# A fused conditional mixing and MXFP4 FFN kernel: 64 x 64 mixing quarters, ScalarE on tile pairs, and a new order on every engine

## The reference

```python
w = weights[conditions]                       # [64, 64, 64]
y = einsum('bct,bcd->bdt', x, w)              # fp32
def quant(x):                                 # blocks of 32 along the last axis
    amax  = max(abs(xb), axis=-1)
    scale = exp2(floor(log2(amax)) - 2)
    q     = clip(xb / scale, -6, 6)
    lsb   = where(|q| < 2, 0.5, where(|q| < 4, 1.0, 2.0))
    return round(q / lsb) * lsb * scale
out = x + einsum('mk,nk->mn', quant(y), quant(W)) + bias    # K = N = 512
```

## Time and profile before

| | us |
|---|---|
| median of three runs | 104.99 |
| the three runs | 103.79, 104.99, 107.01 |
| the profiled execution | 105.2 |
| its span, first to last instruction | 103.7 |
| last residual add starts | 100.39 |
| mean granted TensorE clock | 0.918 of 2.4 GHz |

### The profile page before, as it was taken

How to read it: one execution, slowest core, us unless ns; L and a number is a source line. 1 busy time by engine, 2 the same in 40 slices (tenths; PEclk the granted TensorE clock), 3 DMA queues, 4 the chain that set the end, 5 groups by cost and what they waited for, 6 DMA issues and landing times.

```text
span 103.7 us, 1697 instructions
## 1 busy us (share of the span) xinstructions
PE 82.4 (79%) x434; PEld 40.8 (39%) x440; DVE 91.6 (88%) x149; ACT 79.0 (76%) x113; POOL 28.6 (28%) x50
## 2 busy tenths in 40 slices
PE   5991799904399987996999699699969944899970
PEld 4970334501363435343534534263443413253420
DVE  3579999999996689999999999999999999999660
ACT  3840299869774999999999999999999997903400
POOL 3368999664485203000300300030020003000000
PEclk9999859999556999999999999999999998558999
DMA  2898989999998840967994696689387775949855
GB/s 29 313 340 200 340 229 397 344 275 307 318 230 280 292 149 20 234 179 282 236 190 173 231 190 120 242 239 206 127 299 152 152 270 172 213 102 339 328 209 197
DMA packets 13820, 23.70 MB, mean 229 GB/s; under 512 B 3815, under 2 KB 4339, under 8 KB 13812
## 3 DMA queue, kind: packets, MB, share of 16 engines
q1 hardware_dynamic: 11508, 17.83, 50.7%
q0 software_dynamic: 2016, 5.26, 24.9%
q10 hardware_dynamic: 288, 0.52, 1.9%
HBM read 10.49 MB, written 8.39 MB: 182 GB/s over the span
## 4 chain that ended last, share of the span: by engine, by line
DVE 63%; PE 18%; issue 6%; DMA 5%; ACT 4%; SPq 1%; DVEq 0%; ACTq 0%
DVE n_int L507 14%; DVE a L528 9%; DVE top L519 9%; DVE low L494 7%; PE o_ps L268 5%; DMA w_sb<-in_L_ffn_weight_dram 5%; DVE m L455 4%; PE y_ps L244 4%; DVE inv L499 4%; PE y_ps L268 3%; DVE m L461 3%; PE o_ps L257 2%; DVE amax L472 2%; DVE s L478 2%; DVE s L489 2%
## 5 line engine op out<-in xcount | busy, mean ns | idle before, releaser
L244 PE MATMUL y_ps<-x_sb,mix 128*128 128x512 f32 x64 | 33.5, 658 | 6.2 <-ACT y_sb L357 3.4
L268 PE MATMUL o_ps<-wT,aT 128*128 128x512 bf16 x106 | 26.7, 399 | 0.5 <-issue 0.3
L365 ACT ACTIVATE zone<-inv 128x2048 int16<-128x2048 int16 (+1 forms) x10 | 17.4, 1746 | 5.9 <-DVE inv L499 5.8
L349 ACT ACTIVATE z<-y_ps 128x512 bf16<-128x512 bf16 x32 | 18.7, 625 | 2.7 <-PE y_ps L244 2.2
L244 PEld LDWEIGHTS y_ps<-x_sb,mix 128*128 128x128 f32 x64 | 12.7, 210 | 18.5 <-issue 17.6
L157 POOL DMA_DIRECT2D mix<-in_L_cond_weights_dram x32 | 17.1, 539 | 9.7 <-issue 8.6
L507 DVE TENSOR_TENSOR n_int<-y_sb,inv 128x1024 int16<-128x1024 f32 x16 | 19.0, 1222 | 0.8
L227 POOL DMA_DIRECT2D x_sb<-o_sb x6 | 5.3, 880 | 47.5 <-ACT o_sb L373 47.5
L357 ACT COPY y_sb<-y_ps 128x512 f32<-128x512 f32 x32 | 18.1, 605 | 0.0
L268 PEld LDWEIGHTS o_ps<-wT,aT 128*128 128x128 bf16 x112 | 10.7, 101 | 14.5 <-issue 4.1
L257 PE MATMUL o_ps<-ident,a 128*128 128x128 bf16 x128 | 9.3, 231 | 8.4 <-DVE a L528 8.4
(11 more groups left out here) (39 smaller groups left out, 56.0 us busy)
## 6 DMA issues: line engine op xcount, KB each, us to landing
x_sb<-in_x_dram SPq DMA_DIRECT2D x7, 1024.0 KB, 6.9
x_sb<-o_sb POOLq DMA_DIRECT2D x6, 768.0 KB, 5.7
out_dram<-x_sb SPq DMA_DIRECT2D x6, 768.0 KB, 3.5
out_dram<-x_sb SPq DMA_DIRECT2D x14, 256.0 KB, 2.6
x_sb<-in_x_dram SPq DMA_DIRECT2D x2, 512.0 KB, 6.5
w_sb<-in_L_ffn_weight_dram ACTq DMA_DIRECT2D x2, 256.0 KB, 2.9
w_sb<-in_L_ffn_weight_dram SPq DMA_DIRECT2D x2, 256.0 KB, 4.3
mix<-in_L_cond_weights_dram POOLq DMA_DIRECT2D x32, 16.0 KB, 4.8
```

Source lines behind the costliest of these rows:

```text
L244: nc.tensor.matmul(y_ps[:, t, :], mix[:, (step - 1) * GROUP + t, :], x_tiles(step, t), start=True, stop=True).then_inc(y_ready, 1)
L268: last = nc.tensor.matmul(o_bank(step, t), aT[:, t, c, :], wT[:, c, :], start=False, stop=(c == KC - 1))
L349: nc.scalar.activation(blocked(z[:, step % 2, t, :]), permuted_high(y_ps[:, t, :]), ACT.Abs, scale=ZONE_GAIN).then_inc(z_ready, 1)
L365: nc.scalar.activation(zone[:, t0:t0 + n, :].bitcast(I16), inv[:, t0:t0 + n, :].bitcast(I16), ACT.Copy, bias=float(EXPONENT), scale=-1.0). ...
```

## The change

1. **Mixing.** `mix` holds only the 64 x 64 matrices, without cleared corners. `mix_pair` makes four products of 64 x 64 for each pair of tiles, one on each quarter of the array; results of the off-diagonal quarters land in the other half of the partitions, so within a pair of tiles two samples change places. The transposes of `turn_pair` put them back, by writing their columns in 2 x 64 pieces.
2. **ScalarE** takes z and y in pairs of tiles, 1024 elements. All quantisation tensors are laid out by sub-block first, then tile. In the loop the turned copies come last, and the first copy out comes right behind the zone.
3. **VectorE.** `highest_zone` is gone; its limit comes from `lowest_zone` (the constants move by two binades, and W's scale factor from 0.25 to 4). The tree of step s+1 is interleaved with the rounding of step s, and the add stands behind `lowest_zone`.
4. **FFN.** `ffn_pair` starts as soon as the first two tiles are turned, with two bias matmuls each time. Both mixing pairs follow, before the transposes.
5. **Prologue.** 24 warm-up rounds, the bias loaded as 16 x 32 by GpSimd, its four small VectorE steps set among those of W, twelve one-row transfers instead of four of three rows, and no memsets of `mix`.
6. **Tail.** The residual of step 7 is added on TensorE: `residual_pair` multiplies x by an identity, again in quarters, into the bank of the output. ScalarE copies the result to `x_sb` and the store puts exchanged samples right. Step 8 does not exchange. VectorE adds step 8 alone.

No matmul is put in to keep TensorE busy while it waits.

```diff
-                nc.tensor.matmul(y_ps[:, t, :], mix[:, (step - 1) * GROUP + t, :], x_tiles(step, t),
-                                 start=True, stop=True).then_inc(y_ready, 1)
+        QUARTERS = ((0, 0), (1, 1), (0, 1), (1, 0))
+        HALVES = (slice(0, C), slice(C, P))
...
+                for i, (r, g) in enumerate(QUARTERS):
+                    n = 2 * q + g
+                    mixed = y_ps[HALVES[r], n, :] if step == LAST else y_ps[HALVES[g], 2 * q + r, :]
+                    last = nc.tensor.matmul(mixed, mix[HALVES[r], (step - 1) * GROUP + n, :],
+                                            x_tiles(step, n)[HALVES[r], :], start=True, stop=True)
+            def residual_pair(step, q):
+                for r, g in QUARTERS:
+                    nc.tensor.matmul(o_bank(step, 2 * q + r)[HALVES[g], :], ident_f[HALVES[r], :],
+                                     x_tiles(step, 2 * q + g)[HALVES[r], :], start=True, stop=False)
+            def ffn_pair(step, q):
+                pe.wait_ge(aT_ready, tiles_done(step, 2 * q + 1))
+                if q == 0 and 1 < step < LAST - 1:
+                    pe.wait_ge(added, adds_before(step))
+                for t in (2 * q, 2 * q + 1):
+                    bias_tile(step, t, start=(step != LAST - 1))
+                for t in (2 * q, 2 * q + 1):
+                    ffn_tile(step, t)
...
-                highest_zone(step + 3)
...
+                nc.vector.tensor_tensor(a2[:, t:t + n, :].rearrange("p t (h k) -> p h t k", h=HI),
+                                        columns(n_int, t, n).rearrange("p h (t k) -> p h t k", k=COLS),
+                                        columns(top, t, n).rearrange("p h (t k) -> p h t k", k=COLS), ALU.mult
...
-            nc.gpsimd.memset(mix[C:P, 2 * GROUP:TILES, 0:C], 0.0).then_inc(lower_clear, 1)
-            nc.gpsimd.memset(mix[0:C, 2 * GROUP:TILES, C:P], 0.0).then_inc(upper_clear, 1)
...
+            copy_late(0)
+            copy_turned_last(0)
+            copy_turned_last(1)
+            copy_late(1)
+            copy_turned_last(2)
+            copy_turned_last(3)
```

More of the change, by code:

```diff
@@ L278, in ffn_group, with keep_busy @@
                     ffn_tile(step, t)
+            def keep_busy(times):
+                for i in range(times):
+                    c = i % KC
+                    nc.tensor.matmul(o_ps[:, 2, c * P:(c + 1) * P], idle[:, :], idle[:, :], start=True, stop=True)
             pe.wait_ge(idle_ready, 1)
             with pe.Fori(0, WARMUPS) as _:
[L282 to L285 removed]
@@ L525, in rescale @@
+            def rescale(step, done, rounded, t=0, n=GROUP):
+                if step > 0 and t == 0:
                     dve.wait_ge(t_ready, GROUP * step)
@@ L574, in _ @@
             rescale(0, 1, 2)
-            tree_1(1, 3)
-            tree_2(3)
-            tree_3(3)
+            tree_1(1)
+            tree_2(4)
+            tree_3(4)
             block_max(3)
             lowest_zone(3)
-            highest_zone(3)
-            lift(1, 3)
-            top_zone(2)
+            lift(1, 3).then_inc(z_used, 1)
+            top_zone(3)
             invert(2)
             for step in range(1, LAST):
+                if step > 1:
+                    tree_1(step + 1)
@@ L599, in _ @@
-                lift(step + 1, step + 3)
-                top_zone(step + 2)
-                invert(step + 2)
-            for half in range(2):
-                round_y(LAST, half)
-                limit(LAST, LAST + 1 + half, 2 * half, 2)
-                rescale(LAST, LAST + 1 + half, 2 * LAST + 1 + half, 2 * half, 2)
-            for step in DVE_STEPS:
-                for t in range(GROUP):
-                    add_residual(step, t)
+                if step == 1:
+                    tree_1(step + 1)
+                    limit(step, step + 1)
+                    tree_2(step + 4)
+                    rescale(step, step + 1, 2 * step + 2)
+                    tree_3(step + 4)
+                    block_max(step + 3)
+                    lowest_zone(step + 3)
+                else:
+                    tree_3(step + 4)
+                    limit(step, step + 1)
+                    block_max(step + 3)
+                    rescale(step, step + 1, 2 * step + 2)
+                    lowest_zone(step + 3)
+                    add_residual(step - 1, 0)
@@ L612 @@
+                lift(step + 1, step + 3).then_inc(z_used, 1)
+                top_zone(step + 3)
+                invert(step + 2)
+            for q in range(2):
+                round_y(LAST, q)
+                limit(LAST, LAST + 1 + q, 2 * q, 2)
+                rescale(LAST, LAST + 1 + q, 2 * LAST + 1 + q, 2 * q, 2)
+            for t in range(GROUP):
+                add_residual(LAST, t)
 _INS = ["x", "itok_B_1_198", "L0_cond_weights", "L0_ffn_weight", "L0_ffn_bias"]
```

500 lines of the change are left out of this document (243 added, 257 removed).

## The result

The changed kernel takes **108.63 us** (median of 4 runs, 108.04 to 109.89), the kernel before 104.96 beside it (4 runs, 103.79 to 107.01): a ratio of 1.037, 95% interval 1.022 to 1.052. Forecast was 103.6 us, a little faster than before. It is slower, by 3.7%; the stated range of 99 to 113 holds the time, but the change went the other way. Some executions of every kernel here come out one to four per cent longer at a lower granted clock; the ratios leave them out and the medians do not, so a ratio can differ from the quotient of two medians.

What follows compares the result with a forecast made beforehand. It took VectorE and ScalarE as full before, and a 9.64 us ScalarE-TensorE loop after. 105.2 less 4.0 gave 101.2, 101.0 at the median; plus 2.6 for the clock made 103.6 us, range 99 to 113.

Steps and rivals of the forecast that it cites:

- The loop: Steady step through ScalarE and TensorE, from turned copy through FFN and copies to the next: 9.64 us, 0.35 more than before.
- Quartered mixing: TensorE's mixing in 64 x 64 quarters: between 0.86 us a pair and 3.87 us for two pairs; the lower bound was taken.
- the forecast's case: Quarters run side by side on TensorE, clock lost now and then: 103.6 us, between 101.5 and 106, chance 0.38.
- The second rival: TensorE's quarters go in order, two at a time, so the loop runs through mixing at 11.27 us: 112.8 us, chance 0.22.
- 28.7 + 5 x 9.64: Start of step 6's first turned copy: step 1's at 28.7 us plus five equal loops, 76.9 us against 77.3 before.
- Sum at full clock: 96.4 - 100.39: Shift in the start of the last residual add, -4.0 us, taken off the profiled execution's 105.2 to give 101.2.
- The clock: TensorE's rests of 2.2 us a step lose the clock one and a half times at 1.7 us: +2.6 us, bounds 0 to 8.5.
- VectorE: Without highest_zone and with the new order, VectorE's work falls by 0.4 to 8.9 us a step; layouts cost nothing.
- both engines full: VectorE and ScalarE were both busy for the whole 9.29 us step, so a gain on one alone is worth little.
- Prologue: Start of the kernel: invert(0) ends at 11.3 us, and step 1's first turned copy starts at 28.7 instead of 28.79.
- Tail: From step 7's FFN, starting at 86.2 us, to the last residual add at 96.4 instead of 100.39.
- step 7 at full clock: Step 7's first turned copy, after residual quarters and transposes on TensorE, starts at 85.1 us instead of 86.62.

Runs made afterwards that it cites:

- experiment 3: The changed kernel with ScalarE's two turned copies ahead of the y copy of tiles 0 and 1: 100.43 us, ratio 0.963 to the kernel before.
- experiment 5: The changed kernel with every step mixed, transposed and its residual added on the two diagonal quarters, no exchange, stores of 128 partitions for step 7: 116.02 us.
- experiment 9: experiment 3 with step 8 mixed on four quarters, transposes restoring samples, straight stores, and step 7's residual behind its transposes: 99.51 us, ratio 0.944.
- experiment 7: The kernel before with VectorE's part alone: highest_zone gone, next step's tree around the rounding, add behind lowest_zone: 123.04 us, ratio 1.168.
- experiment 8: The kernel before with highest_zone taken out and nothing moved: 104.23 us against 105.88, no ratio.
- experiment 1: The changed kernel with 32 filling matmuls on an empty tile behind each step's transposes: 106.86 us, ratio 1.026 to the kernel before.
- experiment 2: The changed kernel with 32 filling matmuls behind the transposes of steps 1 to 6, none in step 7: 106.74 us, ratio 1.015.
- experiment 4: The changed kernel with the turned copies ahead of the y copy and twelve filling matmuls in each step: 100.91 us, ratio 0.965.
- experiment 6: The changed kernel with the two upper-half stores of step 7's four 64-partition stores issued by GpSimd instead of SyncE: 108.91 us, ratio 1.034.
- experiment 11: experiment 10 with twelve filling matmuls behind the transposes of steps 1 and 2 alone: 98.89 us, ratio 0.935 to the kernel before.
- experiment 10: experiment 9 with step 7's residual in two parts, the first eight products ahead of the transposes: 97.99 us, ratio 0.927.

## Why the prediction was wrong

The forecast was 101.2 us for the profiled execution at full clock, and 2.6 for the clock. It came to 108.08. Against the full-clock sum the 6.9 us split so: prologue -0.7, five loops +4.1, step 7 +1.8, tail -0.2, end and outside the span +1.9. By its own steps:

**The loop** was right in its mechanism and 0.19 short in its size: 9.83 for 9.64. Of this 0.11 lies between turned copy and copy out (4.72 for 4.61), 0.08 behind it. Five times that is 0.95; another 0.35 lies in the first two loops (9.90 and 10.11). 0.3 of it stands in the second loop between the FFN matmul that the copy out waits for (done at 42.53) and the copy out (42.92); the profile shows no wait there, and its cause stays open. ScalarE's wait (0.96 for 1), VectorE's in front of `limit` (1.04 for 0.75) and the rest on TensorE (2.04 for 2.2) were where it put them. In the steady steps of experiment 3 the first is gone, the second 0 to 0.43 and the third 1.13. The forecast priced the loop at +0.35 a step. It also made TensorE's rest long, and one y copy set behind the turned copies gave back both, 0.91 a step and the clock.

**Quartered mixing**: the forecast's case held, four at once (1.09 us for a pair, two passes of 0.6 and 0.48 between their starts). The second rival, by which quarters go in order, is out: it priced both pairs at 3.87 us, and they take 1.09 each. The Trainium skill (TensorE: Matmul & The Clock Gate, Part 3, The mechanism) says that matmuls start and end strictly in program order; but it says as well that products on different tiles of the array overlap, and the prediction drew on the first alone. This trace agrees with the overlap: the kernel writes the four products of a pair one after another, and their first passes start within 0.02 us of each other (53.43 to 53.45 us), 0.46 ahead of the first of the second passes. In what order the passes were issued no view shows, so the trace does not decide whether they kept to it.

**Failed step 1: "all steps alike" in "28.7 + 5 x 9.64".** Step 8 is mixed without exchange, on two quarters, and the fifth loop holds that mixing: 3.65 us instead of 2.5, and z waits 0.35 and 0.67. The step took 10.99, +1.16. The line `if step == LAST` stood in the diff that the prediction quoted. It had even stated, for the rival, what two passes on the same quarter cost, and that mixing decides once both pairs take more than 2.24 us. Experiments 5 and 9 show it from both sides: with early copies the fifth loop takes 10.07 on two quarters (experiment 3) and 8.91 on four (experiment 9), and with two quarters in every step each undisturbed one takes 10.99 (experiment 5).

**Failed step 2: the sum ended at the last add.** "Sum at full clock: 96.4 - 100.39" took what lies behind the add as unchanged. It grew by 1.7 us. Two things changed there. Step 7 is now stored by four transfers that read 64 partitions each. And SyncE's program reaches them later: ahead of them stands the store of step 6's tiles 1 to 3, which waits until GpSimd's accumulating transfer has landed. That transfer, then that store in the changed kernel and in the kernel before (timelines of GpSimd and SyncE):

```profile
89.30 0.87 POOL L252 DMA_DIRECT2D x_sb<-o_sb  x1 [11.71 <-ACT o_sb L421]
```

```profile
95.09 0.37 SPq L188 DMA_DIRECT2D out_dram<-x_sb  x1
```

```profile
92.12 0.37 SPq L169 DMA_DIRECT2D out_dram<-x_sb  x1
```

The computing behind it became shorter, so this store is issued 6.3 us ahead of the last add instead of 8.3, and it and all of steps 7 and 8, 2816 KB, still have to go out. The same times in every profiled execution (the kernel before and its kin, experiments 7 and 8, store step 7 tile by tile, the others in pairs):

| kernel | stores of step 7 | store of step 6 issued | last add | span ends | store to end | add to end |
|---|---|---|---|---|---|---|
| changed | 64 partitions | 95.09 | 101.39 | 106.4 | 11.3 | 5.0 |
| experiment 1 | 64 | 93.19 | 98.84 | 104.3 | 11.1 | 5.5 |
| experiment 2 | 64 | 93.50 | 97.89 | 104.7 | 11.2 | 6.8 |
| experiment 3 | 64 | 86.94 | 92.72 | 98.2 | 11.3 | 5.5 |
| experiment 4 | 64 | 87.66 | 92.53 | 99.1 | 11.4 | 6.6 |
| experiment 6 | 64, two queues | 95.76 | 102.08 | 106.9 | 11.1 | 4.8 |
| experiment 11 | 128 | 87.89 | 94.38 | 98.6 | 10.7 | 4.2 |
| experiment 8 | 128 | 91.60 | 98.02 | 101.9 | 10.3 | 3.9 |
| experiment 10 | 128 | 85.98 | 93.10 | 96.2 | 10.2 | 3.1 |
| experiment 5 | 128 | 101.88 | 109.33 | 112.5 | 10.6 | 3.2 |
| before | 128 | 92.12 | 100.39 | 103.7 | 11.6 | 3.3 |
| experiment 9 | 128 | 88.24 | 97.00 | 100.2 | 12.0 | 3.2 |
| experiment 7 | 128 | 109.30 | 119.40 | 122.7 | 13.4 | 3.3 |

With half stores the end follows the store of step 6, 11.1 to 11.4 us behind it, wherever the last add lies. With stores of 128 partitions it comes 3.1 to 3.3 us behind the last add where that store is issued 7.1 us or more ahead of it, and later where it is not: 4.2 and 3.9 us at 6.5 and 6.4. So the form of the stores explains a part only. An estimate from the table: with stores of 128 partitions, and the 10.3 to 10.7 us from store to end of experiments 8 and 11, the changed kernel would have ended at 105.4 to 105.8, 4.0 to 4.4 us behind its last add. 0.6 to 1.0 of the 1.7 us are then the half stores, the rest the late store of step 6. The nearest pair, experiments 6 and 11, agrees: with that store 6.3 and 6.5 us ahead of the last add the end lies 4.8 and 4.2 us behind it. No experiment changed the form of the stores and nothing else, and why a store of half the partitions drains slowly was not taken apart.

**The clock** was a term of the right kind and somewhat too small: 1.61 in the loop from step 4 to step 5 and 1.6 from step 6 to step 7, 3.2 in all, for 2.6. Experiment 1 gives 3.1 back. That rests of 2 us lie between those that lose the clock and those that don't held: in the profiled executions the clock fell in two of the five FFNs behind such a rest, and in experiment 3, with 1.13, in none.

**VectorE** was right in that its gain was worth little, and wrong in why: "both engines full". ScalarE set 9.29 alone (experiment 8). The layouts cost nothing: the three-level write of a2 takes 1.22 us, as `lift` does in the earlier trace rows. The prediction did not price VectorE's new order as a wait; experiment 7 shows that in the old arrangement the new order, tree and add together, costs 18 us.

**Prologue**: invert(0) ended at 10.27, forecast 11.3; the first turned copy at 28.02, forecast 28.7. VectorE's and ScalarE's first rows, timeline:

```profile
9.58 0.69 DVE L535 TENSOR_SCALAR inv<-low 128x2048 int16<-128x2048 int16 x1
...
10.30 1.91 ACT L413 ACTIVATE zone<-inv 128x2048 int16<-128x2048 int16 x1 [3.62 <-DVE inv L535]
```

The slow instruction beside the memset of the earlier trace rows is gone, as forecast; how the gain splits among the changes of the prologue was not taken apart. **Tail**: 11.08 from turned copy to last add, forecast 11.3; it was 13.77. That gain is what brought the last add nearer to the store of step 6.

So of the 4.3 us between 103.8 (101.2 + 2.6) and 108.08, two terms near the program's end that never entered the sum make 1.2 and 1.9; the loop's size 0.95, the first two loops 0.35, the clock 0.6 and step 7 at full clock 0.2 were each a little short; the prologue and the tail gave 0.9 back. The second of them alone undoes the 1.4 us that were forecast as a gain (105.2 - 103.8). That the range of 99 to 113 holds the time is owed to its width, which was drawn for other cases.

## What to carry to other kernels

When every engine's work shrinks, write down the loop through all of them in program order: here one y copy in front of the turned copies, where it hid nothing, cost more than all the saved work was worth, and behind them it was free. Follow the special cases of a change (the last step, the other store form) with the same care as the loop, to the last byte that lands: a tail that computes faster gains nothing if the oldest store in its queue is released no sooner. And before an order is carried over to one engine alone, ask what the moved instruction waits for and what stands behind it.

## What the runs showed of the hardware

- Products of 64 x 64 on four different quarters of TensorE's array run side by side in fp32: eight passes in 1.09 us, where eight on two quarters take 1.93 (experiment 10).
- The last four stores of 256 KB took a median of 2.5 us to land in experiment 10 and 3.6 in experiment 11, both with stores of 128 partitions; where half stores of 64 partitions were among the late ones, these took 4.2 (SyncE) and 4.8 (GpSimd) (experiment 6).
- In six kernels with half stores the span ended 11.1 to 11.4 us behind the issue of step 6's store, while its distance to the last add went from 4.8 to 6.8 us. Removing the filling from step 7 moved the last add 0.95 us forward (98.84 to 97.89), but that store went from 93.19 to 93.50 and the end from 104.3 to 104.7.
